# Gathering the edges' attributes plainly in a four-part graph network kernel

## The reference, cut to what matters

```python
src = node_in[edge_src]
a0, a1 = edge_attr[:, 0:1], edge_attr[:, 1:4]
out0 = alpha * (einsum('ei,io->eo', s0 * a0, w_00_0) + inv_sqrt3 * einsum('eim,em,io->eo', s1, a1, w_11_0))
out1 = alpha * (einsum('ei,io,em->eom', s0, w_01_1, a1) + einsum('eim,io->eom', s1 * a0[:, :, None], w_10_1))
messages = msg_ang * msg_rad      # msg_rad: one number per edge, from edge_attr_10
agg = segment_sum(messages, edge_dst, num_segments=N)
```

## Time and profile before

| | |
|---|---|
| median of three executions | 5620.3 us (5606.59 to 5629.95) |
| span of the profiled execution, first to last instruction | 5234.5 us, 64530 instructions |
| its own whole time | not listed apart; the median is 385.8 us above the span |
| busy: PE, DVE, ACT, POOL | 3992.0, 2746.1, 1847.6, 3710.0 us |
| attribute gathers (L916) | 416, 655.4 us busy |

### The profile page before, as it was taken

One profiled execution on the slowest core, in us unless ns is written; L12 is line 12 of the kernel. 1 busy time (PEld: TensorE's weight loads), 2 busy tenths in 40 slices (PEclk: granted clock), 3 DMA queues, 4 the chain that ended last, 5 costly groups with the idle time before them and its releaser, 6 DMA issues.

```text
span 5234.5 us, 64530 instructions
## 1 busy us (share of the span) xinstructions
PE 3992.0 (76%) x17691; PEld 3086.9 (59%) x17691; DVE 2746.1 (52%) x6371; ACT 1847.6 (35%) x5458; POOL 3710.0 (71%) x3085
## 2 busy tenths in 40 slices
PE   4565554667985655699796777789999999988886
PEld 3443343445664433466464444468888888877886
DVE  6476667885436555888532888850010002235555
ACT  1154444663334444577232222120000000046665
POOL 4477778888887777888888777788888800037775
PEclk8878777998987777799897888889999999989998
DMA  8699995663339999576423777746666655557676
GB/s 261 200 328 334 329 324 131 161 161 45 31 56 338 338 337 312 132 168 144 75 21 54 208 211 207 178 89 154 153 141 139 149 152 151 153 146 198 198 200 164
DMA packets 734961, 951.33 MB, mean 182 GB/s; under 512 B 277381, under 2 KB 526260, under 8 KB 734472
## 3 DMA queue, kind: packets, MB, share of 16 engines
q1 hardware_dynamic: 419634, 538.30, 34.0%
q0 software_dynamic: 298192, 385.84, 31.5%
q10 hardware_dynamic: 16774, 23.00, 1.2%
HBM read 727.03 MB, written 219.80 MB: 181 GB/s over the span
## 4 chain that ended last, share of the span: by engine, by line
POOL 36%; PE 23%; issue 19%; DMA 16%; SPq 3%; DVE 2%; POOLq 0%; ACT 0%; DVEq 0%
POOL arena L863 24%; PE bank L2443 21%; POOL ATT L900 6%; POOL sc L886 6%; DMA sc<-arena 4%; DMA ATT<-arena 4%; DMA VE<-arena 4%; DMA arena<-KVT,arena 3%; SPq L574 2%; DMA arena<-X1T,arena 1%; PE bank L2152 1%; SPq L570 1%; PE bank L2477 1%; DVE arena L1027 0%; PE bank L2428 0%
## 5 line engine op out<-in xcount | busy, mean ns | idle before, releaser
L2443 PE MATMUL bank<-arena 128*128 128x256 f32 x5000 | 1101.8, 380 | 1.7 <-DVE arena L1686 1.2
L2443 PEld LDWEIGHTS bank<-arena 128*128 128x128 f32 x5000 | 945.5, 190 | 131.4 <-DVE arena L1686 2.0
L863 POOL DMA_INDIRECT arena<-KVT,arena x832 | 808.6, 972 | 278.2 <-issue 239.9
L2287 PE MATMUL bank<-arena 128*128 128x264 f32 x1664 | 606.0, 529 | 453.8 <-ACT arena L1892 439.4
L863 POOL DMA_INDIRECT arena<-YT,arena x416 | 422.9, 1017 | 568.6 <-DMA YT<-arena 442.1
L2287 PEld LDWEIGHTS bank<-arena 128*128 128x128 f32 x1664 | 419.8, 264 | 639.3 <-issue 546.8
L916 POOL DMA_INDIRECT arena<-ATTR,arena x416 | 655.4, 1575 | 144.9 <-issue 144.9
L900 POOL DMA_INDIRECT ATT<-arena x391 | 642.0, 1642 | 130.6 <-issue 110.6
L886 POOL DMA_INDIRECT sc<-arena x391 | 642.5, 1643 | 123.8 <-issue 111.9
L2244 PE MATMUL bank<-arena 128*128 128x273 f32 x1664 | 455.3, 412 | 141.1 <-DVE arena L1406 117.9
L863 POOL DMA_INDIRECT arena<-X1T,arena x416 | 420.4, 1011 | 126.9 <-issue 123.2
(11 more groups left out here) (309 smaller groups left out, 5462.0 us busy)
## 6 DMA issues: line engine op xcount, KB each, us to landing
VE<-arena SPq DMA_DIRECT2D x208, 512.0 KB, 5.8
arena<-VE SPq DMA_DIRECT2D x208, 512.0 KB, 3.6
arena<-ATT SPq DMA_DIRECT2D x250, 320.0 KB, 3.0
arena<-AM SPq DMA_DIRECT2D x250, 320.0 KB, 2.9
ATT<-arena POOLq DMA_DIRECT2D x25, 1600.0 KB, 6.6
arena<-LOCT SPq DMA_DIRECT2D x312, 128.0 KB, 5.4
arena<-ATT SPq DMA_DIRECT2D x75, 384.0 KB, 4.3
AM<-arena SPq DMA_DIRECT2D x100, 256.0 KB
```

The lines of the kernel that those rows point to most:

```text
L863: GP.indirect_dma_start(out=ring[:, i % n, k, :], out_offset=None, in_=table, in_offset=bass.IndirectOffsetOnAxis(ap=idx[:, 4 * i + k:4 * ...
L2287: mm = P.matmul(b_[:, 0:264], OHQ[:, i % 3, k * 128:(k + 1) * 128], QS[:, i % 4, k, :], start=True, stop=True)
L2443: mm = P.matmul(bank[j][:, 0:256], left[:, 128 * j:128 * (j + 1)], right[:, u, :], start=(u == 0), stop=(u == W - 1))
```

## The change

The attribute gathers lose the addition and the check of the index against the table's size, so that they overwrite numbers 2 to 5 of each place in `PA` instead of adding onto them; and the clearing of these numbers in preparation goes. The index of a chunk is in number 0, which the gather does not write. Nothing else differs.

```diff
         for c in range(T):
             GP.indirect_dma_start(
                 out=PA[:, c, 2:6], out_offset=None, in_=ATTR,
-                in_offset=bass.IndirectOffsetOnAxis(ap=PA[:, c, 0:1].bitcast(I), axis=0), bounds_check=R1 - 1,
-                compute_op=ALU.add).then_inc(attr_back.sem, 16)
+                in_offset=bass.IndirectOffsetOnAxis(ap=PA[:, c, 0:1].bitcast(I), axis=0)).then_inc(attr_back.sem, 16)
...
         d.then(V.tensor_copy(PA[:, :, 0].bitcast(I), PA[:, :, 2]))
-        d.mark(V.memset(PA[:, :, 2:6], 0.0))

         V.wait_ge(*small_out("prep", asked[0]))
```

## The result

| | before | changed |
|---|---|---|
| median, first comparison | 5620.1 us (5606.6 to 5630.0) | 6115.2 us (6112.3 to 6117.1) |
| ratio | | 1.0875, 95% interval 1.0860 to 1.0891 |
| span of a recorded execution | 5234.5 us (ahead), 5621.2 us (recorded again) | 6111.2 us |

The change costs 8.75%. But times have to be read by session here: the kernels of one session run one after the other on one chip, the kernel before among them. In four sessions of this study, and in the first comparison, the kernel before took 5619 to 5650 us; in three others it took 5239 to 5244 us, and there the change does nothing. The trace ahead of the prediction is of the second kind, the times beside it of the first. I call them sessions with and without hold-ups.

The account below looks back on a forecast made before the run. POOL's indirect gathers and PE's hops were taken to bound the kernel, the attribute gathers hidden before the hops' end at 4643.7. Terms of -0.1, 0, 0 +- 3.5 and 0 +- 0.6 us gave 5620 us, range 5596 to 5640.

Parts of the forecast that it names:

- The reference for the sum: Whole kernel: effects summed on the recorded span of 5234.5 us, with the median of 5620.3 lying 385.8 us above it.
- around the span: Outside the recorded span: 385.8 us assumed there, nothing tied to the edit, at most 2.5 us from fewer instructions.
- The end of l1: Landing of the last X1T gather, with attribute gathers right behind: 0 us, +-3.5 us for more or less crowding.
- Traffic beside the hops: 0 us: PE's hops beside the attribute gathers: denser gathers leave the pace at 0.216 us a matmul, 0 +- 0.6 us.
- Rival 1: Hops beside the gathers: loads of LEFT are crowded out, some 110 us slower, 5730 us; chance 0.05.
- The rule beside rival 1: DMA engines take turns between queues packet by packet, so many small gather packets could push back the hops' big loads.
- The gathers' time on POOL: Attribute gathers, L916: 1.30 us each instead of 1.92, ending near 3943 instead of 4201.6; 0 us on the path.
- wait for YT near 700: POOL's idle wait at L863 behind the attribute gathers grows from 442 us to about 700.
- Readers, moves, memset: DVE and ACT reading attributes, POOL's 29 ns MOVEs, the clearing at L1222: 0 us each, 0.1 us gained on POOL beside the memset.

Follow-up runs that it names:

- the moved kernel: Changed kernel, with POOL starting the attribute gathers only once the hops' first projection is taken over for all windows: 6171.7 us beside 5643.8 before, in a session with hold-ups.
- the memset of 512: Changed kernel with a POOL memset of 128x512 ahead of each plain attribute gather, one in 1.72 us: 5634.9 us beside 5619.5 before.
- that of 160: Changed kernel with a POOL memset of 128x160 ahead of each plain attribute gather, one in 1.42 us: 6004.0 us beside 5619.5 before.

## Why the prediction was wrong

- **The reference for the sum** is the step that failed first. The prediction put the 385.8 us between median and span "around the span" and argued on from the trace. They were inside the timed executions, 358 us of them beside plain gathers. All its rows, and the bounds from them, came from a session in which the mechanism does not show. The kernel before, recorded again, has time and span 1.2 us apart.
- **What denser gathers do to the others** is what the sum put at nothing. "The end of l1" had 0 +- 3.5 us and came to +177 us with hold-ups. The projections with the hops' first part, between l1's end and the stretch from which the rows of the hops were read, had no term at all and came to +324 us. Without hold-ups both are within 0.5 us of the trace ahead. The prediction looked for an effect in bytes and landing times; the harm goes by the number of gathers in a microsecond, and POOL's pace was taken as a gain only.
- **"Traffic beside the hops: 0 us"** came out as 0 in the changed kernel (1117.6 us in all three traces above), but by luck of place: the hops behind their first part had not begun when the gathers ended. Where the gathers were moved beside them they cost 528 us (1646.1 against 1117.6).
- **Rival 1** had the direction and the place that would be hit in the moved kernel, but the wrong mechanism, and got 0.05. SP issued 22 loads instead of 255 there, not because packets crowded them out but because PE freed their places late. Its price, 110 us, was far too low, and its sign, loads that take over 8.6 us to land, would not have shown the cause.
- **The rule beside rival 1**, the turns between queues packet by packet of the Trainium skill (DMA: Bandwidth & Descriptors, "Queues, rings and completion order"), is not what does the harm here: 143 packets a gather at one in 1.92 us do next to none, 31 at one in 1.34 us do. No run here tests the rule itself.
- **The gathers' time on POOL** was right: 1.30 us forecast; 544.6/415 = 1.31 without hold-ups and 1.34 with them. Last gather near 3943, measured 3950.6; wait for YT near 700, measured 696.8. The 0.6 us that no row split is the addition, but for 0.03 us.
- **Readers, moves, memset** at 0 us each: nothing contradicts it. The memset kept gives 6129.6 us beside 6123.6 and 6115.2 without it, in kernels that differ from each other by as much.
- **The end of l1, +-3.5 us,** is right without hold-ups (35.9 us against 36.0, and 1243.6 us for the whole stretch against 1243.3).

What stays open is what PE and the gathers share. Two things point to the profiler's own records. First, they are lost in the sessions with hold-ups: of the 6656 landings of the attributes the trace holds 659 in the changed kernel, 4395 before, 4011 with the memset of 512, 1171 with that of 160, but 6644 in a session without hold-ups; and of all changes of semaphores each trace with hold-ups holds 47522 to 52253 records, each trace without hold-ups 92750 or more. Second, single instructions of PE that send no signal are held up too. The Trainium skill (NOTIFIC — the notification-queue block, "Overflow: three behaviours, one of which stalls the engine") says that in one of its settings the block drops records when the ring in memory is full, and that its internal pipeline holds its producers back rather than lose one. A block that writes its records out more slowly in some sessions than in others would give both signs. No run here shows it: every timed execution here comes with a span, so none is known to run without records. Whether the 9% would be there without a profiler is not known, nor what sets the sessions apart.

## What to carry to other kernels

Ask a trace first whether it is of the same kind as the times: a span that is 7% under the median is a finding, and no sum stands on it until it is explained. An instruction off the critical path has a second cost beside its duration, the rate at which it and its landings come; a slower form of it (here the adding gather at one in 1.9 us) may be what keeps the rest moving, and an engine that runs far ahead of its deadline (442 us here) gains nothing from more speed. Where a row of small POOL gathers must stay, spacing them is worth a try only if other engines show idle times that no work of theirs explains: with hold-ups a pause of 0.55 us took 480 us off the changed kernel's time, without them pauses ahead of 832 gathers cost 1.4%. Times that were taken with a profiler running don't tell whether either holds without it.

## What the runs showed of the hardware

- Plain gathers of POOL at one in 1.34 us hold up PE, and through it every engine that waits for PE, in some sessions; at one in 1.72 us they don't. Rows a gather (32 or 128) do not matter.
- While held up, PE's signals leave in order at one instruction in 1.40 us (43.6 and 53.1 us late instead of 0.04), while ACT's signal to PE and the landings that POOL waits for come in time. Kept at it, PE does 185 products in 530 us, at a granted clock of 0.50.
- An addition in a gather of 128 rows of 16 bytes costs POOL 0.55 to 0.6 us, a check of the bounds 0.03 us. Without the addition a gather is moved in some 31 packets instead of 143, with 32 rows as with 128.
